# One step of a cross-attention block: which engines add the two parts of probabilities times values

## The reference

```python
def _L0_xattn_ref(hidden_states, memory_tokens, memory_mask, norm_w, wq, wk, wv, wo, wg):
    x = rmsnorm(hidden_states, norm_w)
    q = (x @ wq.T).reshape(B, L, NH, HD)
    k = (memory_tokens @ wk.T).reshape(B, M, NH, HD)
    v = (memory_tokens @ wv.T).reshape(B, M, NH, HD)
    attn = jnp.einsum('blhd,bmhd->bhlm', q, k) * scale
    attn = jnp.where(memory_mask[:, None, None, :], attn, -jnp.inf)
    attn = jax.nn.softmax(attn, axis=-1)
    attn = jnp.nan_to_num(attn, nan=0.0)
    out = jnp.einsum('bhlm,bmhd->blhd', attn, v).reshape(B, L, C)
    out = out @ wo.T
    gate = jax.nn.sigmoid(x @ wg.T)
    return gate * out

x = x + jnp.tanh(g_xattn[0]) * _L0_xattn_ref(_layernorm(x, axis=-1), ctx_2048, mask_BxS2_bk0, ...)
x = x + jnp.tanh(g_ffn[0]) * _L0_ffn_ref(_layernorm(x, axis=-1), ...)
```

## Time and profile before

| what | value |
|---|---|
| time, median of 3 runs | 596.18 us (595.61 to 596.45) |
| profiled execution: time | 596.42 us |
| profiled execution: span from first to last instruction | 594.6 us |
| granted TensorE clock, mean | 0.986 |
| PE busy | 542.4 us, 91% |
| DVE busy | 463.7 us, 78% |
| ACT busy | 336.8 us, 57% |
| POOL busy | 273.5 us, 46% |

### The profile page before, as it was taken

The page is one execution under the profiler, slowest core; times in us unless marked ns, Lnnn a source line. Parts: engine busy times, 40 slices in busy tenths (PEclk is TensorE's granted clock), DMA queues, the critical chain, the costliest instruction groups (busy, mean ns, idle before and its releaser), DMA issues.

```text
span 594.6 us, 12502 instructions
## 1 busy us (share of the span) xinstructions
PE 542.4 (91%) x3962; PEld 472.7 (80%) x3962; DVE 463.7 (78%) x1063; ACT 336.8 (57%) x936; POOL 273.5 (46%) x308
## 2 busy tenths in 40 slices
PE   2888999999899998999998898989999999999996
PEld 1787878788788887888876676878988978899983
DVE  6665989768898688996657998998898899876721
ACT  3777566444665446654467636666666666765610
POOL 6922352202532024330115745766766676776720
PEclk9897999899999999999999999999999999999998
DMA  7930146332453323423671028302110211011111
GB/s 225 331 110 1 54 150 177 139 98 79 146 163 129 119 85 116 134 89 95 228 295 33 1 73 291 119 1 80 37 36 1 81 36 36 2 36 36 37 62 31
DMA packets 27899, 59.37 MB, mean 100 GB/s; under 512 B 3656, under 2 KB 5832, under 8 KB 27848
## 3 DMA queue, kind: packets, MB, share of 16 engines
q1 hardware_dynamic: 27848, 58.76, 30.2%
HBM read 39.62 MB, written 19.14 MB: 99 GB/s over the span
## 4 chain that ended last, share of the span: by engine, by line
PE 50%; DVE 24%; issue 11%; ACT 7%; POOL 6%; DMA 1%; DVEq 1%; SPq 0%; ACTq 0%; POOLq 0%
PE bank L1737 12%; PE bank L1750 11%; PE bank L322 8%; PE bank L1586 5%; PE bank L1614 3%; PE bank L1590 2%; DVE part_gate L1361 2%; POOL hT_lo L770 2%; PE bank L331 2%; DVE nmax L1158 2%; DVE vb_both L1126 2%; ACT probs L896 2%; DVE hidden L1376 2%; DVE part_up L1361 2%; POOL part_up L783 2%
## 5 line engine op out<-in xcount | busy, mean ns | idle before, releaser
L1737 PE MATMUL bank<-mT_hi,wgu 128*128 128x320 f32 x440 | 139.7, 327 | 15.1 <-DVE part_up L1361 5.2
L1737 PE MATMUL bank<-mT_lo,wgu 128*128 128x320 f32 x440 | 131.5, 309 | 0.0
L718 POOL TENSOR_TENSOR o<-pv_sum,rinv 100x128 f32<-100x128 f32 x64 | 47.4, 741 | 162.0 <-DVE pv_sum L1175 161.7
L896 ACT ACTIVATE probs<-bank,nmax 100x96 f32<-100x96 f32 x256 | 66.2, 344 | 73.4 <-DVE nmax L1158 73.1
L1737 PEld LDWEIGHTS bank<-mT_hi,wgu 128*128 128x128 f32 x440 | 82.5, 188 | 31.6 <-DVE part_up L1361 8.1
L1737 PEld LDWEIGHTS bank<-mT_lo,wgu 128*128 128x128 f32 x440 | 82.8, 188 | 3.5
L993 ACT ACTIVATE part_up<-bank,scale 128x320 f32<-128x320 f32 x110 | 57.2, 521 | 46.7 <-PE bank L1737 46.7
L777 POOL TENSOR_TENSOR part_gate<-part_gate 128x320 f32<-128x320 f32 x55 | 57.1, 1038 | 51.6 <-DVE part_gate L1361 51.6
L1361 DVE SCALAR_TENSOR_TENSOR part_up<-bank,scale,part_up 128x320 f32<-128x320 f32 x110 | 58.4, 544 | 19.2 <-ACT part_up L993 18.1
L993 ACT ACTIVATE part_gate<-bank,scale 128x320 f32<-128x320 f32 x110 | 52.3, 528 | 27.3 <-PE bank L1737 27.1
L783 POOL TENSOR_TENSOR part_up<-part_up 128x320 f32<-128x320 f32 x55 | 57.1, 1037 | 22.9 <-DVE part_up L1361 21.2
(11 more groups left out here) (145 smaller groups left out, 1407.5 us busy)
## 6 DMA issues: line engine op xcount, KB each, us to landing
gate_up_scratch<-left SPq DMA_DIRECT2D x12, 512.0 KB, 6.4
down_scratch<-left SPq DMA_DIRECT2D x12, 512.0 KB, 3.4
wgu<-gate_up_scratch SPq DMA_DIRECT2D x11, 512.0 KB, 6.2
words<-in_packed SPq DMA_DIRECT2D x18, 256.0 KB
xn<-in_x SPq DMA_DIRECT2D x16, 200.0 KB
xa<-in_x SPq DMA_DIRECT2D x16, 200.0 KB
x_scratch<-gate SPq DMA_DIRECT2D x16, 200.0 KB
ctx_raw<-in_ctx_tail SPq DMA_DIRECT2D x4, 768.0 KB, 8.0
```

The costliest lines, as they stand in the source:

```text
L718: nc.gpsimd.tensor_tensor(o[hg % 2][:, :, HD * h:HD * h + HD], total[:, :, 0:HD], rinv[:, i % 4, :].unsqueeze(2).broadcast_to([L, NB, HD]) ...
L896: last = nc.scalar.activation(probs[i % 2][:, cols], SC[i % HPG][0:L, cols], ACT.Exp, bias=nmax[:, i % 4, b:b + 1])
L1737: last = nc.tensor.matmul(product_bank(j, t, i, k)[:, 0:TG], wgu[t][:, k, 128 * i:128 * i + 128], mT[j % 2][half][:, k, :], start=half == ...
```

## The change

ACT now copies both halves of the bank in one instruction (2 x 136 columns) into `pv_copy`, which has two buffers. DVE makes only the reciprocal, from the copy. POOL makes the addition, which was DVE's, and then the multiplication as before. The next attend waits for the copy (`s_pvlow`) and no longer for the sum. ACT's copy into a buffer waits for the sum and the reciprocal of two steps before, and DVE's reciprocal waits for the `o` of four steps before (it was two).

```diff
-        pv_low = sb(phase_a, "pv_low", [L, NB * VW], F32)
+        pv_copy = [sb(phase_a, f"pv_copy{s}", [L, 2, NB * VW], F32) for s in range(2)]
...
                 n, hg, h = STEPS * g + i, i // HPG, i % HPG
                 total = pv_sum[i % 2][:, :].rearrange("t (b w) -> t b w", w=VW)
+                pool.wait_ge(s_pvlow, n + 1)
+                hi, lo = (pv_copy[i % 2][:, half, :] for half in range(2))
+                nc.gpsimd.tensor_tensor(pv_sum[i % 2][:, :], hi, lo, ALU.add).then_inc(s_pvsum, 1)
                 pool.wait_ge(s_inv, n + 1)
                 pool.wait_ge(s_pvsum, n + 1)
                 nc.gpsimd.tensor_tensor(o[hg % 2][:, :, HD * h:HD * h + HD], total[:, :, 0:HD],
...
                 act.wait_ge(s_pv, n + 1)
-                if not isinstance(n, int) or n:
-                    act.wait_ge(s_pvsum, n)
-                nc.scalar.activation(pv_low[:, :], PV[0:L, PV_LOW:PV_LOW + NB * VW], ACT.Copy).then_inc(s_pvlow, 1)
+                if not isinstance(n, int) or n >= 2:
+                    act.wait_ge(s_pvsum, n - 1)
+                    act.wait_ge(s_inv, n - 1)
+                nc.scalar.activation(pv_copy[i % 2][:, :, :], PV[0:L, :].rearrange("t (a w) -> t a w", a=2)[:, :, 0:NB * VW], ACT.Copy)\
+                  .then_inc(s_pvlow, 1)
...
-            def attn_sum(g, i):
+            def attn_inverse(g, i):
...
                 dve.wait_ge(s_pvlow, n + 1)
-                if not isinstance(n, int) or n >= 2:
-                    dve.wait_ge(s_on, n - 1)
-                pv = PV[0:L, 0:NB * VW].rearrange("t (b w) -> t b w", w=VW)
+                if not isinstance(n, int) or n >= 4:
+                    dve.wait_ge(s_on, n - 3)
+                pv = pv_copy[i % 2][:, 0, :].rearrange("t (b w) -> t b w", w=VW)
                 nc.vector.reciprocal(rinv[:, i % 4, :].unsqueeze(2), pv[:, :, HD:HD + 1]).then_inc(s_inv, 1)
-                nc.vector.tensor_tensor(pv_sum[i % 2][:, :], PV[0:L, 0:NB * VW], pv_low[:, :], ALU.add).then_inc(s_pvsum, 1)
...
-                    pe.wait_ge(s_pvsum, n)
+                    pe.wait_ge(s_pvlow, n)
```

More of the change, by code:

```diff
@@ L1199, in step @@
                 if not isinstance(g, int) or g or i:
-                    attn_sum(*last_step(g, i))
+                    attn_inverse(*last_step(g, i))
                 if i % HPG == SCORES_AT:
@@ L1447, in _ @@
                     if part_of == "H":
-                        attn_sum(GROUPS - 1, STEPS - 1)
+                        attn_inverse(GROUPS - 1, STEPS - 1)
                     elif part_of == "T3":
```

## The result

| | before | after |
|---|---|---|
| time, median | 595.97 us (595.61 to 596.45, 4 runs) | 602.75 us (600.16 to 603.23, 4 runs) |
| ratio, 95% interval | | 1.0093 (1.006 to 1.0126) |
| profiled execution: time, span | 596.42, 594.6 us | 602.56, 600.8 us |
| granted TensorE clock, mean | 0.986 | 0.970 |
| PE, DVE, ACT, POOL busy | 542.4, 463.7, 336.8, 273.5 us | 551.4, 457.9, 344.6, 299.6 us |

What follows compares the result with a forecast made beforehand. PE was taken as bound by its own queue, with 9.9 us of waits on DVE and POOL in the loop. Gain 4.0 less 1.35 less 0.3 gave 2.35 us: 594.0 us forecast, range 591.3 to 597.5.

Steps and rivals of the forecast that it cites:

- T2: Job before the scores of step 14; predicted to wait 0.3 to 0.4 us for POOL's `o`, covered by idle time.
- the wait for `oT_lo`: PE's wait for DVE before score matmuls in the loop; predicted to fall from 6.4 to some 4 us.
- The tie of the earlier trace: DVE's line 1114 takes 1.82 us behind POOL's `wo_lo`, begun 0.01 us earlier; reversed, an estimated 1.1 us gained.
- rival 3: No stall counts, the end is even and line 1114 no longer waits for `wo_lo`: 591.3 us, chance 0.10.
- The sign that was named for rival 1: DVE's decoding stages or `xn` taking longer than before; each stall was put at 0.83 us.
- rival 1: POOL's additions keep DVE out of SBUF: two stalls of 0.83 us a turn give 597.8 us; chance 0.15.
- rival 2: POOL's backlog in steps 10 to 13 is 0.5 us worse and starves PE: 596.0 us, no change; chance 0.17.
- seven on the chain in each turn: 4.0 us: Loop: removing seven DVE additions on the chain, 0.19 us each, gains 4.0 us over three turns.
- The charge of 0.45 a turn for POOL: Loop: POOL collisions lose 0.2 us each at steps 6 and 8, plus 0.05 for steps 10 to 13.
- I charge 0.3 for the whole end: End of the attention, beside the first FFN tiles: 0.3 us lost, between 0.6 gained and 0.7 lost.
- the 1.2 us that the prediction allows for noise: Whole kernel: the measurement was taken to tell about 0.2%, 1.2 us, from no change.

Runs made afterwards that it cites:

- e3: Kernel before with DVE's addition cut from 136 columns to 4, the other 132 left out and nothing given to POOL; median 597.0 us.
- f3: Kernel before with one more POOL addition of 100 x 136 in every step, its result unused, DVE keeping its own; median 599.2 us.
- g1: Changed kernel, but in the last group's last ten steps ACT copies 136 columns and DVE adds again; median 601.0 us.
- e4: Changed kernel with a DVE reduction of 136 columns in SBUF put in front of its reciprocal; median 607.0 us.
- g3: g1 with 14 and 12 small matmuls a turn filling PE's two waits at the scores of step 2; median 592.7 us, ratio to before 0.9918.
- h3: g3 repeated unaltered in another set of executions; median 596.5 us, ratio to before 0.9951.
- f2: Kernel before with 14 and 12 small matmuls a turn filling PE's two waits at the scores of step 2; median 597.4 us, ratio 1.0003.

## Why the prediction was wrong

- **Right: the pieces.** The copy takes 398 ns (0.40 predicted), the reciprocal 168 (172), the addition 478 (430); T2 waits 0.17 us for `o` (0.3 to 0.4); the wait for `oT_lo` is 3.8 us (some 4). The tie of the earlier trace rows stands as it was, 1.84 us, so rival 3 had no ground. The sign that was named for rival 1 did show, in small: step 6's decoding instruction took 0.78 us for 0.68, step 8's `xn` 0.67 for 0.54, and the longest decoding instruction of a turn 1.11 for 0.92. It cost the loop nothing that shows, and rival 2 did not appear: between the falls the changed kernel is level or gains through every turn.
- **The step "seven on the chain in each turn: 4.0 us" was mis-sized.** It counts 0.19 us for each of seven additions, 1.33 a turn. e3 takes 0.14 of each and gets 0.47 a turn, about half of 0.97; scaled up to the whole 0.19, an estimate, that is 0.6. The chain shows who is last, addition by addition, but not how much of it PE can use before its own queue is last. The charge of 0.45 a turn for POOL was too high as well: the changed kernel's turn is 0.62 us shorter, all that the estimate allows, and f3's is as long as before's. Net: 0.62 a turn for 0.88. The 16 steps up to the first step 2 inside the loop gained 0.75 (67.25 us against 68.00 in f3, with a fall at about the same place in both). All together 2.0 us for 2.65.
- **The step "I charge 0.3 for the whole end" failed.** It cost 1.5: 1.0 up to step 63 and 0.5 at the last hand-over, both shown by g1, which gets them back. The prediction had the mechanism and the rows, but took as its price the length of the added instruction (0.43). The price is that of all that POOL does without a gap once DVE has come too late.
- **No step spoke of the clock: the sum took it as the same in both kernels, and the time as known to 0.2%.** This is the step that put the result outside the range. At equal clock the balance is 2.0 - 1.5, so 0.5 us faster; measured +0.3 ± 0.4, level. The 6.8 us of the result are 6.7 us of clock by the line (0.986 to 0.970). Part of this is the draw: four executions of before near its good end, and 1.7 us lost in after's trace before the first attend. Against the 1.2 us that the prediction allows for noise, one unchanged kernel spreads over 13.8 us. Part is the change: its clock is 0.0044 ± 0.0017 lower on average over 16 and 120 executions, 1.8 us. So the rival that decided is one I did not have: TensorE's clock falls behind two idle gaps of PE, and in the changed kernel's loop it does so more often. That the gaps' new lengths are the reason is not shown; e3 and e4 speak against it as the only one. The Trainium skill, TensorE: Matmul & The Clock Gate, section on HAM oscillation, describes waits that throw the clock back in each pass of a loop. The changed kernel's traces agree, with 1.5 or 3.1 us for each, though its waits are short ones for DVE, and the page's are long ones for DMA. The same page, Part 1, puts the warm-up at below 1% of a typical span; here, with the falls further in, the kernel before alone moves by 2.3%.

## What to carry to other kernels

When a change shortens waits of PE, read the granted clock of the stretch behind each wait that remains, and set times against the mean clock of each execution before a difference of 1% is believed. Where a loop leaves PE idle for about a microsecond at one place, a few matmuls of nothing there can be worth more than the work that was moved: g3 and h3 together lie 3.7 ± 0.6 us below before, of which the moved work has about 2. It is to be measured each time, for in f2 the same matmuls gained nothing that is clear of noise. An engine that shares SBUF with DVE should be given work only where it has gaps: price a collision by the whole run of its instructions without a gap, not by the added one, and treat parts of the program (loop and end) apart.

## What was not expected of the hardware

- One unchanged program on one core took 592.5 to 606.3 us in 120 executions, and its mean granted clock (0.964 to 0.995) explains all but a scatter of 1.1 us.
- Two waits of 0.68 and 0.48 us, 0.36 us of matmul apart, were followed by half clock in 15 turns of 15, in the traces of five executions; two of 0.81 and 0.41 us in 6 of 15.
- 26 matmuls of 0.045 us in these gaps kept the clock full behind them in 12 turns of 12, and none of the 44 executions with them has a mean clock of 0.972 or less.
